# An attention and feed-forward layer on one core: two steps at a time on every engine, eight places for rotated heads

## What is computed

```
c_q = h @ w_down_q.T;  c_kv = h @ w_down_kv.T          # 128 -> 64 each
q, k = rope(c_q @ w_up_q.T), rope(c_kv @ w_up_k.T)     # 16 heads of 64
attn = softmax(q @ k.T / 8);  v = c_kv @ w_up_v.T
out = (attn @ v) @ w_out.T + xn
# spikes: y = relu(xn @ W_fc.T)**2 @ W_proj.T, a threshold neuron run 5 steps on y, spikes / 5
```

## Time and profile before

| | |
|---|---|
| median of 3 runs | 1083.32 us (1083.18 to 1086.99) |
| profiled execution, its time | 1083.63 us |
| its span, first to last instruction | 1081.8 us |
| TensorE busy | 1041.4 us (96%) |
| ScalarE, VectorE, GpSimd busy | 930.0, 898.9, 895.9 us |

### The profile page before, as it was taken

The page is one execution under the profiler, slowest core; times in us unless marked ns, Lnnn a source line. Parts: engine busy times, 40 slices in busy tenths (PEclk is TensorE's granted clock), DMA queues, the critical chain, the costliest instruction groups (busy, mean ns, idle before and its releaser), DMA issues.

```text
span 1081.8 us, 26191 instructions
## 1 busy us (share of the span) xinstructions
PE 1041.4 (96%) x6880; PEld 700.7 (65%) x6880; DVE 898.9 (83%) x1223; ACT 930.0 (86%) x3136; POOL 895.9 (83%) x897
## 2 busy tenths in 40 slices
PE   3789999999999999999999999999999999999987
PEld 2556666666666666666666666666666666666654
DVE  3798888898888889888889888889888888888872
ACT  3789988988998888999898999898899889898861
POOL 3777989888888888888898888988888988888851
PEclk9899999999999999999999999999999999999999
DMA  5388777877877877777887777787777787777773
GB/s 178 106 227 207 204 209 202 223 211 200 205 208 204 230 203 207 206 202 202 219 215 207 203 203 209 201 228 208 199 208 206 203 229 204 210 195 196 207 193 81
DMA packets 93281, 217.96 MB, mean 201 GB/s; under 512 B 22464, under 2 KB 43200, under 8 KB 93120
## 3 DMA queue, kind: packets, MB, share of 16 engines
q1 hardware_dynamic: 92864, 216.52, 75.5%
q10 hardware_dynamic: 384, 1.05, 0.4%
HBM read 7.77 MB, written 4.19 MB: 11 GB/s over the span
## 4 chain that ended last, share of the span: by engine, by line
PE 80%; issue 6%; DVE 6%; SPq 3%; ACT 2%; DMA 2%; ACTq 0%; DVEq 0%; POOL 0%; POOLq 0%
PE ps_s L328 20%; PE ps_u L342 20%; PE ps_b L447 10%; PE ps_qk L318 8%; PE ps_a L383 5%; PE ps_a L396 5%; PE ps_qk L319 4%; SPq L254 3%; PE ps_b L413 2%; DVE turned L703 2%; DVE qk L687 2%; PE ps_a L355 1%; PE ps_a L360 1%; PE ps_b L456 1%; PE ps_a L367 1%
## 5 line engine op out<-in xcount | busy, mean ns | idle before, releaser
L538 ACT ACTIVATE prob<-ps_s,neg_max 128x256 f32<-128x256 f32 x1024 | 475.0, 486 | 41.0 <-DVE neg_max L692 38.2
L837 POOL TENSOR_TENSOR partner<-partner,rope_sb 128x512 f32<-128x512 f32 x256 | 327.1, 1278 | 108.3 <-DMA partner<-raw 108.3
L692 DVE TENSOR_REDUCE neg_max<-ps_s 128x4 f32<-128x1024 f32 x256 | 310.8, 1214 | 116.9 <-PE ps_s L328 115.4
L840 POOL TENSOR_TENSOR qk<-qk,partner 128x512 f32<-128x512 f32 x256 | 326.5, 1275 | 20.1
L703 DVE STREAM_TRANSPOSE turned<-prob 128x1024 f32<-128x1024 f32 x256 | 316.4, 1236 | 2.3 <-ACT prob L538 1.3
L328 PE MATMUL ps_s<-qk 64*128 64x256 f32 x2048 | 292.4, 404 | 3.5 <-ACT prob L538 2.4
L342 PE MATMUL ps_u<-gathered,ckv 128*64 128x256 f32 x2048 | 278.4, 393 | 3.1 <-DMA gathered<-turned 2.8
L328 PEld LDWEIGHTS ps_s<-qk 64*128 64x128 f32 x2048 | 177.5, 187 | 106.0 <-issue 86.5
L538 ACT ACTIVATION_READ_ACCUMULATOR prob<-ps_s,neg_max 128x1 f32 x1024 | 221.8, 217 | 0.0
L550 ACT COPY raw<-ps_qk 128x512 f32<-128x512 f32 x256 | 154.1, 602 | 67.0 <-PE ps_qk L319 66.9
L342 PEld LDWEIGHTS ps_u<-gathered,ckv 128*64 128x64 f32 x2048 | 124.8, 136 | 107.8 <-issue 52.6
(11 more groups left out here) (67 smaller groups left out, 897.5 us busy)
## 6 DMA issues: line engine op xcount, KB each, us to landing
gathered<-turned SPq DMA_DIRECT2D x1016, 128.0 KB, 2.4
partner<-raw SPq DMA_DIRECT2D x256, 256.0 KB, 2.4
x_sb<-in_x SPq DMA_DIRECT2D x32, 128.0 KB, 2.3
resid<-early SPq DMA_DIRECT2D x32, 128.0 KB, 2.0
out<-out_sb SPq DMA_DIRECT2D x32, 128.0 KB, 2.1
turned<-in_wup SPq DMA_DIRECT2D x2, 512.0 KB, 5.7
gathered<-turned ACTq DMA_DIRECT2D x8, 128.0 KB, 4.0
rope_sb<-in_rope SPq DMA_DIRECT2D x1, 512.0 KB, 6.8
```

What stands on the lines that cost most here:

```text
L538: last = nc.scalar.activation(prob[:, s % 2, :, h, :, t, :].rearrange("p j k c -> p k j c"), ps_s[:, s % 2, h, t, :].rearrange("p (k j c) ...
L692: nc.vector.tensor_reduce(neg_max[:, s % 2, :, :], ps_s[:, s % 2, :, :, :], AXIS_X, ALU.max, negate=True).then_inc(max_ready, 1)
L837: nc.gpsimd.tensor_tensor(other, other, sin_sb, ALU.mult).then_inc(sin_ready, 1)
L840: nc.gpsimd.tensor_tensor(qk[:, s % 4, :, :], qk[:, s % 4, :, :], other, ALU.add).then_inc(rope_done, 1)
```

## The change

Every engine's `step` now handles steps g and g+1 (a **pair**; an item has four, `q` = 0 to 3). TensorE does the scores of both, the first projection, a part of the full-array work, the second projection, the rest of the full-array work, and the weighted latents of both into the two halves of the bank `ps_u`, which ScalarE copies out in one instruction of 512 columns where it had two of 256. The leads become `project` 14, `rope` 12, `scores` 8, and `turn` goes with `scores` (g+8), where it was one step behind. The ring `qk` has 8 places where it had 4. SP issues all 16 DMAs of a `move` together behind the exchange, where it had 4 ahead of an exchange and 12 behind it. In the last steps ScalarE issues its 8 DMAs of the last group in one piece, ahead of the copy of the row sums.

```diff
-LEAD = {"project": 12, "rope": 10, "scores": 8, "turn": 7, "multiply": 0}
+LEAD = {"project": 14, "rope": 12, "scores": 8, "multiply": 0}
+RING = 8
...
-                if (s + turn) % GROUP == GROUP - 1 and not outside(g + turn, STEPS):
-                    move(g + turn, s + turn, (0,))
-                if (s + LEAD["project"]) % 2 == 1 and not outside(g + LEAD["project"], STEPS):
-                    exchange(g + LEAD["project"], s + LEAD["project"])
-                if (s + turn) % GROUP == 0 and not outside(g + turn - 1, STEPS):
-                    move(g + turn - 1, s + turn - 1,
-                         (1,) if isinstance(g, int) and g + turn == STEPS else (1, 2, 3))
+                if not outside(g + LEAD["project"], STEPS):
+                    exchange(i * BODY + ahead, ahead)
+                if last % GROUP == GROUP - 1 and not outside(i * BODY + last, STEPS):
+                    move(i, last, (0, 1) if isinstance(g, int) and i * BODY + last == STEPS - 1 else (0, 1, 2, 3))
...
+                for j in range(2):
+                    for kt in range(TT):
+                        for h in range(2):
+                            last = nc.tensor.matmul(
+                                ps_u[h * L:(h + 1) * L, j * S:(j + 1) * S], ckv[:, (s // PAIRS) % 2, kt, :],
+                                gathered[:, (s // GROUP) % 2, :, (s + j) % GROUP, h, kt, :, :]
+                                .rearrange("p i t r -> p t i r"),
...
+                if q == 0:
+                    if spread:
+                        broadcast_rden(b - 1, 0)
                     if not outside(b + 2, B):
                         latents(b + 2, b0)
                     if not outside(b + 1, B):
                         latents_by_token(b + 1, 1 - b0)
+                elif q == 1:
+                    if spread:
+                        broadcast_rden(b - 1, 2)
+                    if not outside(b, B):
+                        ffn_out(b, 0)
+                        ffn_out(b, 1)
+                elif q == 2:
+                    if spread:
+                        attention_out(b - 1, 0, 1 - b0)
+                        attention_out(b - 1, 1, 1 - b0)
+                    if not outside(b + 1, B):
+                        ffn_in(b + 1, 0, 1 - b0)
+                else:
+                    if not outside(b + 1, B):
+                        ffn_in(b + 1, 1, 1 - b0)
+                    if spread:
+                        attention_out(b - 1, 2, 1 - b0)
+                        attention_out(b - 1, 3, 1 - b0)
+            def behind_second(b, b0, q):
+                if q < 2 and not outside(b - 1, LAST):
+                    broadcast_rden(b - 1, 2 * q + 1)
+                if q == 2 and is_last(b):
+                    broadcast_last_rden(b)
+                if q == 3:
+                    if is_last(b):
+                        last_attention_out(b, 2, b0)
                     if not outside(b + 3, B):
                         transpose_inputs(b + 3, 1 - b0)
+                    if isinstance(b, int) and b == -2:
+                        value_by_output()
+                    if not outside(b - 1, B):
+                        transpose_sum(b - 1)
+                    if not outside(b, LAST):
+                        transpose_rden(b)
...
                 if not outside(g + LEAD["scores"], STEPS):
-                    scores(g + LEAD["scores"], s + LEAD["scores"])
+                    for k in range(2):
+                        scores(g + LEAD["scores"] + k, s + LEAD["scores"] + k)
                 if not outside(g + LEAD["project"], STEPS):
                     project(g + LEAD["project"], s + LEAD["project"], i)
-                extras(b, b0, p)
+                behind_first(b, b0, q)
+                if not outside(g + LEAD["project"], STEPS):
+                    project(g + LEAD["project"] + 1, s + LEAD["project"] + 1, i)
+                behind_second(b, b0, q)
                 if not outside(g, STEPS):
                     weigh_latents(g, s, i)
...
-                nc.scalar.copy(u_sb[:, (s // PAIRS) % 2, pair, :], ps_u[:, 0:S]).then_inc(u_evac, 1)
+                nc.scalar.copy(u_sb[:, (s // PAIRS) % 2, pair:pair + 2, :],
+                               ps_u[:, :].rearrange("p (j s) -> p j s", j=2)).then_inc(u_evac, 1)
...
+                raws, exps = not outside(g + LEAD["project"], STEPS), not outside(g + LEAD["scores"], STEPS)
+                spread = not outside(b - 1, LAST)
+                if q == 0:
+                    if spread:
+                        copy_rden(b - 1)
+                    if not outside(b, B):
+                        square(b, 1)
+                elif q < 3:
+                    if spread:
+                        copy_spread(b - 1, 2 * q - 1)
+                else:
+                    if not outside(b + 3, B):
+                        normalise(b + 3, 1 - b0, 1)
+                if raws:
+                    copy_projected(g + LEAD["project"], s + LEAD["project"], i)
+                if q < 2 and spread:
+                    copy_spread(b - 1, 2 * q)
+                if q == 3 and not outside(b + 1, B):
+                    relu(b + 1, 1)
+                if q == 0 and isinstance(b, int) and b == -1:
+                    copy_value_by_output()
+                if exps:
+                    exponentials(g + LEAD["scores"], s + LEAD["scores"], i)
+                if q == 0 and not outside(b + 2, B):
+                    lead_latents(b + 2, b0)
+                if q == 2 and not outside(b + 1, B):
+                    relu(b + 1, 0)
+                if raws:
+                    copy_projected(g + LEAD["project"] + 1, s + LEAD["project"] + 1, i)
+                if q == 0 and not outside(b + 1, B):
+                    copy_latents(b + 1, 1 - b0)
+                if exps:
+                    exponentials(g + LEAD["scores"] + 1, s + LEAD["scores"] + 1, i)
+                if q == 2 and not outside(b + 3, B):
+                    normalise(b + 3, 1 - b0, 0)
+                if not outside(g, STEPS):
+                    copy_u(g, s, i)
+                if q == 1 and is_last(b):
                     copy_last_rden(b)
+                if q == 3:
+                    if not outside(b + 3, B):
+                        copy_inputs(b + 3, 1 - b0)
                     if not outside(b + 1, B):
+                        square(b + 1, 0)
+                if is_last(b + 1) and q == 3:
+                    move_last(2)
+                    move_last(3)
...
+                ahead, near = LEAD["project"], LEAD["scores"]
+                rotates, turns = not outside(g + ahead, STEPS), not outside(g + near, STEPS)
+                if q == 0 and is_last(b - 1):
                     normalise_last(b - 1, 3, 1 - b0)
+                if q == 0 and not outside(b - 2, B):
                     finish(b - 2, b0, i - 1)
+                if turns:
+                    row_max(g + near, s + near)
+                if q == 2 and not outside(b, B):
+                    for k in (2, 3, 4):
+                        integrate(b, b0, k)
+                if q == 2 and rotates:
+                    rotate(g + ahead, s + ahead)
+                if turns:
+                    row_max(g + near + 1, s + near + 1)
+                if q != 2 and rotates:
+                    rotate(g + ahead, s + ahead)
+                if q == 1:
+                    if not outside(b + 3, B) and not outside(b + 1, B):
+                        moments_of(b + 3, 1 - b0, i + 1 + b0)
+                    if not outside(b, LAST):
+                        invert_sums(b, b0)
+                elif q == 3 and not outside(b - 1, B):
                     add_spikes(b - 1, 1 - b0)
+                if turns:
+                    turn(g + near, s + near, i)
+                if q == 0 and not outside(b + 2, B):
                     split_latents(b + 2, b0)
+                if rotates:
+                    rotate(g + ahead + 1, s + ahead + 1)
+                if q == 1 and not outside(b, B):
+                    for k in (0, 1):
+                        integrate(b, b0, k)
+                if turns:
+                    turn(g + near + 1, s + near + 1, i)
```

176 lines of the change are left out of this document (55 added, 121 removed).

## The result

The kernel with the change takes 1186.28 us (median of 4 runs, 1185.01 to 1188.52) against 1083.71 (4 runs) before: ratio 1.094, 95% interval 1.091 to 1.097. It is 9.4% slower. 1093 was predicted, and 1060 to 1110 as the range.

The account below looks back on a forecast made before the run. TensorE set the pace before; after, one long round per item through TensorE, ScalarE and VectorE would, at 32.1 us. Span 1081.8 + 5.4 + 1.5 + 3 = 1091.7, so 1093 us, range 1060 to 1110.

Parts of the forecast that it names:

- the sum: Per item, four pieces of work one after the other: 16.2 + 8.98 + 4.15 + 2.79 = 32.1 us, against 32.09 before.
- What it adds: Prediction's section on new waits between engines: one long round per item, 32.1 us, with TensorE standing still about 2.3.
- the round: Chain of waits through TensorE, ScalarE, VectorE and TensorE again, once per item, claimed to take 32.1 us.
- The third rival: Swap's DMAs in front of every second exchange come late: 8.0 us of transfer, 1123 us in all; chance 0.12.
- its own rule: For GpSimd's exchange: from 6.2 us of swap transfer on, each further us costs 1 per item, 31 in all.
- Its counter-argument: Against a late swap: the rotated heads are now wanted two pairs after they are made; no size given.
- The saving: Fewer array-shape changes on TensorE in latents, scores and projection: 0.55 us per pair of steps, 2.2 per item.
- the three places named: TensorE waits before q = 0's second projection (0.9 us), q = 1's second scores (0.8) and q = 1's second projection (0.6).
- step 2: Pair q = 0 in the round: scores, first projection, then ScalarE's copies and exponentials until the turn starts, 8.98 us.
- TensorE is the bound again: The round closes faster and TensorE sets the pace: 1024 us fully open, 1058 half open; chance 0.24.
- The ends: Start: six projections ahead of first scores, not four, +5.4 us; end: ScalarE's eight DMAs, +3, bounds 0 and +6.
- The middle's +1.5: Between first scores and last exponentials, about 30 items x 0.05 us = +1.5 us.

Follow-up runs that it names:

- e3: Changed kernel with two of each group's 16 DMAs cut in two, 18 issues for the same bytes: 1228.2 us, ratio 1.135.
- e1_split: Changed kernel, SP's list reordered: eight DMAs behind the turn, eight behind the next pair's exchange, x load, store and residual ahead of DMAs: 1097.2 us.
- e11: Kernel of e5_tail with ScalarE's 0.48 us copy of the first broadcast moved behind the second exponentials: 1090.5 us, ratio 1.005.
- e5_tail: Kernel of e1_split with the last group's eight DMAs that ScalarE issued moved to SP's queue: 1090.8 us, ratio 1.006.
- e4_before_lump: Kernel before the change, with all 16 DMAs of a group in one piece where 12 stood: 1181.2 us, ratio 1.090.
- e2_smallfirst: Changed kernel with x load, store and residual copy moved ahead of the whole 16 DMAs, the exchange still behind: 1166.5 us, ratio 1.076.
- e12: Kernel before the change, with SP's piece of twelve DMAs cut to eight and four put behind the next exchange: 1183.5 us, ratio 1.090.
- e6: Kernel of e1_split with VectorE rotating the first projected pair before the second row maximum in an item's second step too: 1109.0 us.
- e9: Kernel of e5_tail with VectorE's turns one pair later, pairs 7 and 8 ahead instead of 8 and 9: 1156.4 us, ratio 1.066.

## Why the prediction was wrong

**What failed** is a term that the sum does not have: SP's own time. In "What it adds" the round goes through ScalarE, VectorE and TensorE, and SP's step is taken to be free. The third rival (chance 0.12) looked at the right place but priced the wrong thing: 2.1 MB at the DMA engines' rate, 8.0 us of *transfer*. It also took its own rule (one us per item for each us above 6.2) for one us alone: 8.0 less 6.2 is 1.8 us, times 31 items 56 us, so 1149 and not 1123. The lump holds the queue for 10.09 us of *issue*, the load, the store, the residual and the exchange start behind it, and e3 shows that the issues count and not the bytes. The price of an issue stood in the rows, 1.90 us for three; I used it for ScalarE's eight at the end and not for SP's sixteen. With 16 x 0.63 = 10.1 in it, the same rule gives 3.9 x 31 = 121 us more than the forecast, 1214: above the 1186 that came, but on the right side. Its counter-argument, that rotated heads are wanted only two pairs later, is true of the rotated heads: in the loop of the kernel after, TensorE's scores wait only 7.9 us for them. It missed that GpSimd's product for the attention output stands behind the exchanged heads in GpSimd's list. TensorE waits for that product, and the delay comes round to the turn that starts the next lump. Whether a longer lead would help was not tried.

The Trainium skill, DMA: Bandwidth & Descriptors, Issuing engines are not separate DMA queues, says that the time a sequencer takes to initiate a DMA "is usually small relative to the DMA itself". Here the issue isn't small: it holds the queue for 0.63 us, where the 131 KB at the 263 GB/s of the prediction are 0.50 us. (From issue to landing one such DMA takes 2.3 us, by part 6 of the profile's page, but those of a lump overlap, and the issues don't.) The measurement decides.

**What held**, as e1_split shows with the lump gone. The item: 32.01 us, predicted 32.1, against 32.09 before. The saving: 1.88 and 1.93 for the doubled groups, as written. The waits into which it turns: three, at the three places named, about 2.1 us together instead of 2.3, so without them an item would be the predicted 29.9. ScalarE and VectorE idle, VectorE's turn waiting for the exponentials. TensorE's busy share in the loop is 0.95, predicted 0.93. What is not shown is that the walked round is what binds: e11 takes 0.48 us out of its step 2 and the item falls by 0.13, so that the sum comes within 0.1 us of the item may in part be luck. The "TensorE is the bound again" rival is false: with the queue mended the item doesn't fall below 31.88 in any run.

**The ends** were mis-sized. Start: +6.0 (6.4 in e1_split) for +5.4. End: +8.6 (10.2 in e1_split) for +3, above the bound of +6. The bound left out that an issue on ScalarE costs 0.73 there (5.84 for 8; 6.03 in the kernel after), not 0.63. The trace of the kernel before had it: three in 1.90, but the last four in 3.39. It also left out that TensorE works on at the lower clock after idling (below). e5_tail gave 6.4 of it back by the medians, 8.0 in the profiled executions. The middle's +1.5 was nothing: 1022.5 us against 1022.7.

**The loss by parts**: of the 102 us, 87 are the lump (e1_split takes 85.6 of the span back in its profiled execution, the slowest of four, and 89 by the medians); 6 the lead's start; 9 the end, 6 to 8 of them ScalarE's eight DMAs. e4_before_lump has a like price for a lump without the change, 100.2 us of span, in part by the wait for the swap itself. That the change's main idea, fewer changes of the array's shape, gains nothing per item is a second finding and independent of it: the 2.2 us are saved, and the three waits for VectorE and ScalarE take them back.

## What to carry to other kernels

The queue of an engine that only issues DMAs is an engine with a list of its own: count issues times the row's time per issue, see what stands behind them, and look for "SPq" in the chain before and after, because the page's busy bars don't have it. The chain alone isn't enough: in e2_smallfirst it has SPq at 0%, and only the list of waits (GpSimd for the exchange, 145.0 us) shows the queue. A lump of issues has two deadlines, those of the transfers behind it and its own; splitting it gave 7.5% where its deadline had room (e1) and cost 9% where it had none (e12). And where four engines are each busy for 28 to 30 of 32 us (e1_split's loop: 853.9, 803.6, 788.4 and 784.2 of 900), an instruction moved to close one wait can open another: before moving, walk forward along every list until the next gap, as I didn't in e6, e9 and e12.

## What the runs showed of the hardware

- **Issue time.** A DMA of 128 KB from SBUF to SBUF holds the queue of its engine for 0.63 us (10.09 for 16, 11.35 for 18). With both queues issuing, at the end of e1_split, eight take 5.84 on ScalarE's (0.73 each) and 5.58 on SP's from 1057.75 on (0.70 each; the first five start about 0.6 apart, the later ones 0.7 to 1.0). In e5_tail SP alone issues sixteen there, 0.63 apart again. That the other queue is the reason is not certain: single issues of 1.4 to 2.0 us also occur while the other queue is silent, as the last of the four in the kernel before.

  An exchange of two takes 1.15, an x load 0.39.
- **TensorE's clock after a pause.** In e1_split's tail, by windows (the column behind the busy times is the granted clock), and TensorE's timeline in the last of them:

```profile
1050.00:1057.00 7.00, 6.37 (x42) 4.27 (x39) 5.47 (x6) 4.48 (x19) 0.00 (x0) 1.00 0.81 183
1057.00:1064.00 7.00, 0.00 (x0) 0.00 (x0) 1.23 (x3) 1.30 (x3) 0.00 (x0) 0.81 0.74 180
1064.00:1071.00 7.00, 5.79 (x22) 3.01 (x22) 0.00 (x0) 2.08 (x5) 1.68 (x3) 0.50 0.73 157
```

```profile
1066.42 3.68 PE L347 MATMUL ps_u<-gathered,ckv 128*64 128x256 f32 x16
```

  After the idle 7.28 us the clock is 0.50 (1.2 GHz of 2.4), and the latents take 3.68 us instead of 1.95. A pause costs its length and then the slower work behind it. It need not be so long: e5_tail's latents at 1059.16 take 3.63 us, after waits of 1.59 and 0.77 with two short matmuls behind each, and its windows are:

```profile
1056.00:1059.00 3.00, 0.74 (x4) 0.56 (x4) 1.25 (x3) 2.55 (x5) 0.20 (x1) 1.00 0.36 81
1059.00:1062.70 3.70, 3.70 (x18) 1.77 (x17) 0.00 (x0) 0.00 (x0) 1.47 (x3) 0.54 0.90 203
```

  So e5_tail's gain is not that of the clock alone. In e9, with a wait of 1.2 to 1.5 us ahead of the latents, the clock of the whole loop was 0.96. It was 1.00 in the kernel after, though TensorE was busy for less there (790 of 900 us against 813), so idle time in all doesn't decide it.
